# Where the causal mask enters the scores: a product on TensorE, or a copy into the bank by ScalarE

## What is computed

```
q = rmsnorm(q, q_norm_w); k = rmsnorm(k, k_norm_w)
q = apply_rope(q, cos, sin); k = apply_rope(k, cos, sin)
scores = einsum('bhqd,bhkd->bhqk', q, k) * scale
scores = where(causal, scores, finfo.min)
attn = einsum('bhqk,bhkd->bhqd', softmax(scores), v)
hidden = hidden + attn.reshape(B, S, Hq * hd) @ o_w.T
```

## Time and profile before

| | us |
|---|---|
| median of 3 runs | 1182.44 |
| lowest, highest | 1181.94, 1184.58 |
| the profiled execution, its own time | 1183.33 |
| span of the profiled execution, first to last instruction | 1181.4 |
| busy in it: PE | 1144.4 (97%) |
| DVE | 745.2 (63%) |
| ACT | 648.6 (55%) |
| POOL | 509.0 (43%) |
| mask products (L2236), 64 of 0.379 each | 24.2 |

### The profile page before, as it was taken

One profiled execution on the slowest core, in us unless ns is written; L12 is line 12 of the kernel. 1 busy time (PEld: TensorE's weight loads), 2 busy tenths in 40 slices (PEclk: granted clock), 3 DMA queues, 4 the chain that ended last, 5 costly groups with the idle time before them and its releaser, 6 DMA issues.

```text
span 1181.4 us, 22702 instructions
## 1 busy us (share of the span) xinstructions
PE 1144.4 (97%) x7726; PEld 1021.7 (86%) x7726; DVE 745.2 (63%) x1633; ACT 648.6 (55%) x1839; POOL 509.0 (43%) x566
## 2 busy tenths in 40 slices
PE   9999999999999999999999999999999999988994
PEld 8989999999999999998997788888888888867894
DVE  4666545335543454358777877677777777777666
ACT  4555444444444444455565676666666666674552
POOL 4111131113111311312237776666787587673572
PEclk9999999999999999999999999999999999999997
DMA  9200000000000002023002009910000100042637
GB/s 334 85 1 1 19 2 18 1 1 1 1 19 1 1 1 90 1 98 117 19 18 72 1 1 274 291 43 1 15 19 6 50 20 19 15 99 75 197 112 234
DMA packets 47267, 70.09 MB, mean 59 GB/s; under 512 B 4279, under 2 KB 39355, under 8 KB 46171
## 3 DMA queue, kind: packets, MB, share of 16 engines
q1 hardware_dynamic: 43747, 60.21, 16.9%
q0 software_dynamic: 3408, 8.43, 2.0%
HBM read 40.24 MB, written 29.30 MB: 59 GB/s over the span
## 4 chain that ended last, share of the span: by engine, by line
PE 88%; DVE 5%; issue 2%; ACT 2%; POOL 1%; DMA 1%; SPq 0%; DVEq 0%; POOLq 0%; ACTq 0%
PE bank L1904 15%; PE bank L1941 11%; PE bank L2094 10%; PE bank L1972 7%; PE bank L2148 7%; PE bank L1914 5%; PE bank L1932 5%; PE bank L2239 4%; PE bank L2174 4%; PE bank L2034 3%; PE bank L2279 3%; PE bank L1922 2%; PE bank L2204 2%; PE bank L2214 2%; PE bank L2310 2%
## 5 line engine op out<-in xcount | busy, mean ns | idle before, releaser
L600 POOL TENSOR_TENSOR p<-p,rinv 128x512 f32<-128x512 f32 x64 | 66.6, 1041 | 403.6 <-DVE rinv L1430 403.6
L947 ACT ACTIVATE p<-bank,nb,rq 128x128 f32<-128x128 f32 x256 | 114.0, 455 | 87.7 <-DVE nb L1659 87.6
L814 ACT ACTIVATE p<-bank,nmax 128x128 f32<-128x128 f32 x256 | 90.8, 366 | 115.7 <-DVE nmax L1418 115.5
L675 POOL TENSOR_TENSOR qr<-qr,rb 128x512 f32<-128x512 f32 x64 | 82.5, 1289 | 72.1 <-DVE rb L1607 70.6
L1426 DVE COPY pt<-bank 128x512 f32<-128x512 f32 x64 | 44.2, 691 | 106.1 <-PE bank L1922 105.4
L1904 PE MATMUL bank<-cur_hi,wqk_hi 128*128 128x512 f32 x256 | 107.7, 421 | 0.0
L1904 PE MATMUL bank<-cur_lo,wqk_hi 128*128 128x512 f32 x256 | 101.0, 394 | 0.0
L1904 PE MATMUL bank<-cur_hi,wqk_lo 128*128 128x512 f32 x256 | 100.8, 394 | 0.0
L823 ACT ACTIVATE o_hi<-bank,bqkv 128x512 fp32r<-128x512 f32 x64 | 44.3, 692 | 95.7 <-PE bank L1932 95.4
L1434 DVE SCALAR_TENSOR_TENSOR o_lo<-bank,bqkv,o_hi 128x512 fp32r<-128x512 f32 x64 | 48.0, 750 | 49.7 <-ACT o_hi L823 49.7
L1941 PE MATMUL bank<-wo_hi,o_hi 128*128 128x256 f32 x256 | 77.5, 303 | 0.3 <-DVE o_lo L1434 0.2
(11 more groups left out here) (280 smaller groups left out, 3740.8 us busy)
## 6 DMA issues: line engine op xcount, KB each, us to landing
token_scratch<-empty SPq DMA_DIRECT2D x1, 17415.0 KB, 64.9
xs<-token_scratch SPq DMA_DIRECT2D x39, 129.0 KB, 2.2
wqk_raw<-in_wqk SPq DMA_DIRECT2D x8, 512.0 KB, 9.2
gate<-gates_scratch SPq DMA_DIRECT2D x8, 512.0 KB, 3.7
got_t<-expert_scratch SPq DMA_DIRECT2D x16, 256.0 KB, 4.7
w_raw<-in_w SPq DMA_DIRECT2D x2, 1408.0 KB, 6.1
xres<-in_x SPq DMA_DIRECT2D x4, 512.0 KB, 8.8
wv_raw<-in_wv SPq DMA_DIRECT2D x8, 256.0 KB, 9.3
```

Of the source, the lines that this page charges most:

```text
L600: nc.gpsimd.tensor_tensor(p1[:, h % 2], p1[:, h % 2], rinv[:, h % 2].unsqueeze(2).broadcast_to([P, GB, T]), ALU.mult).then_inc(a_pn, 1)
L675: nc.gpsimd.tensor_tensor(qr[:, s.u % 2], qr[:, s.u % 2], rb[:], ALU.add).then_inc(g_qr, 1)
L814: last = nc.scalar.activation(p1[:, h % 2, b], bank[3][:, b * T:(b + 1) * T], ACT.Exp, bias=nmax[:, h % 2, b:b + 1], accum_out=rsum[:, h % ...
L947: last = nc.scalar.activation(p2[:, (s.u - 3) % 2, j], bank[3][:, j * T:(j + 1) * T], ACT.Exp, scale=rq[:, (s.u - 3) % 4, j:j + 1], bias=n ...
```

## The change

The product for the mask is gone, and so are the two tables for it (`mask`, `ident_b`) with the two instructions of DVE that made them. ACT copies `mask_f` (float32, 128 columns, read four times by a stride of 0) into `bank[3]` instead, by `lay_mask`. It does so once ahead of the first scores and then right behind the exponentials of each step, after it has waited for its own last exponential. PE waits for `g_mask` where it waited for `g_ex`, and adds the scores onto what lies in the bank. One product is new (128x512, once, in the first step): its result is overwritten, but it marks the columns of the bank as written, so that later products without `start` add.

```
+            def lay_mask():
+                nc.scalar.activation(bank[3][:].rearrange("p (j s) -> p j s", j=REP),
+                                     mask_f[:].unsqueeze(1).broadcast_to([P, REP, T]), ACT.Copy).then_inc(g_mask, 1)
+
             def step(s):
                 n, new_seq = s.n, s.new() and s.kv == 0
+                if s.first and s.u == 1:
+                    act.wait_ge(consts, 6)
+                    act.wait_ge(g_add, 1)
+                    lay_mask()
...
                     last.then_inc(g_ex, 1)
+                    if n - 2 < NG * 4 * GB:
+                        act.wait_ge(g_ex, n - 2)
+                        lay_mask()
...
-                            dve.wait_ge(consts, 6)
-                            nc.vector.tensor_copy(mask[:].rearrange("p (j s) -> p j s", j=REP),
-                                                  mask_f[:].unsqueeze(1).broadcast_to([P, REP, T])).then_inc(g_tab, 1)
-                            nc.vector.tensor_copy(ident_b[:], ident[:]).then_inc(g_tab, 1)
...
                     keys_queries()
+                    if s.first and s.u == 0:
+                        pe.matmul(bank[3][:], cur_hi[:, 0, 0:T], cur_hi[:, 0], start=True, stop=True).then_inc(g_add, 1)
...
-                    if s.had(3):
-                        pe.wait_ge(g_ex, n - 2)
-
-                    pe.matmul(bank[3][:], ident_b[:], mask[:], start=True, stop=False, skip_group_check=True)
+                    pe.wait_ge(g_mask, n - 1)
```

More of the change, by code:

```diff
@@ L168, in program @@
         cos_sin = sb("cos_sin", [P, 2, DH], at=W2 + 44 * KB)
-        mask = sb("mask", [P, REP * T], BF16, at=W2 + 45 * KB)
-        ident_b = sb("ident_b", [P, P], BF16, at=W2 + 46 * KB)
         mask_f = sb("mask_f", [P, T], at=W2 + 46 * KB + 256)
@@ L313, in program @@
             sem(f"g_{x}") for x in ("ka", "rk", "kv", "qr", "rq", "qv", "pn"))
+        g_mask, g_add = sem("g_mask"), sem("g_add")
         w_hi4, w_lo4 = sem("w_hi4"), sem("w_lo4")
@@ L471, in _ @@
             sp.dma_start(w_row[:], ins["w_row"].partition_broadcast(P)).then_inc(d_router, 16)
-            sp.wait_ge(g_tab, 11)
+            sp.wait_ge(g_tab, 9)
             sp.dma_start(xs_dram.rearrange("(j p) d -> p j d", p=P),
@@ L1595, in _ @@
                 ffn1(g, False)
-            dve.wait_ge(g_tab, 6)
+            dve.wait_ge(g_tab, 4)
             def rotate(out_cos, out_sin, src, table, cos_free, sin_free, done):
@@ L1637, in step @@
                     nc.vector.tensor_copy(iota[:], iota_i[:]).then_inc(g_tab, 1)
-                    dve.wait_ge(g_tab, 8)
+                    dve.wait_ge(g_tab, 6)
                     nc.vector.tensor_scalar(e_base[:], iota[:, 0:E], float(CAP), None, ALU.mult).then_inc(g_tab, 1)
                     nc.vector.tensor_copy(code[:], code_i[:]).then_inc(g_tab, 1)
-                    dve.wait_ge(g_tab, 10)
+                    dve.wait_ge(g_tab, 8)
                     nc.vector.tensor_scalar(e16[:], iota[:, 0:E], float(CAP // P), None, ALU.mult)
@@ L1644, in step @@
                     nc.vector.tensor_copy(empty[:, D + 1:DW], code[:, GB:GB + 1]).then_inc(g_tab, 1)
-                    dve.wait_ge(g_tab, 11)
+                    dve.wait_ge(g_tab, 9)
                 if s.u == 7:
```

## The result

The kernel with the copied mask takes 1188.92 us (median of 6 runs, 1186.85 to 1190.83); the kernel before took 1184.01 (6 runs, 1181.94 to 1184.63). The ratio is 1.0046, with 1.0034 to 1.0059 as its 95% interval: **0.46% slower**, about 5.4 us, where I had forecast no change. It is above my range, which ended at 1187.0, also if the ratio is laid on the 1182.44 that I had then (1187.9). The profiled execution took 1188.24 with a span of 1186.4, 5.0 more than before.

What follows compares the result with a forecast made beforehand. The prediction took PE to set the pace, with 0.22 us saved per step; nine gains and losses along the second attention summed to -0.2 us, so a median of 1182.2, no visible change. Range: 1176.0 to 1187.0, 8 in 10.

Steps and rivals of the forecast that it cites:

- E: End of the last row reading the exponentials' sums, which releases the score bank; scores could start 0.79 us after it.
- clamps: Steps where the score bank is late: scores start 0.43 us later than before instead of 0.22 sooner.
- DVE's ring: Loop `sq`, `q_ms`, `o_lo`, `nmax`, `nb`, exponentials: 5.23 us after the change against PE's 5.46, pacing where DVE has extra work.
- term 8: 1026 to 1048 us, routing and steps without projections: two later `sq` and three clamps against 4 products saved, +2.3 us.
- term 5: 845 to 931 us: 13 steps gain 0.22 each, less two clamps of 0.5 and 0.1, -2.3 us.
- term 7: 966 to 1026 us: 9 steps gain 0.22 each, less one clamp of 0.4, -1.6 us.
- 2, to 743: 693 to 743 us, into the second group: two clamps and DVE's later end against 7 products saved, +0.3 us.
- 4, border to the third: 825 to 845 us: routing and input split in DVE's ring (0.63 late), then two slacks under 0.79, +0.7 us.
- 6, border to the last: 931 to 966 us: DVE builds a list, its ring runs 0.63 longer twice, against 4 products saved, +1.4 us.
- ACT's ring sets the pace everywhere: Rival: copy at its upper bound, 0.9 with wait, makes the ring 5.48, over PE's 5.46: 1186.7 us, chance 0.17.
- The cover holds: Rival: group borders absorb the delay, only first group and end lose, 51 steps keep 0.22: 1175.2 us, chance 0.18.
- term 9: Behind the last scores: `wd_hi` stands behind a copy and the experts' first work waits for it, +0.2 us.

Runs made afterwards that it cites:

- second pair: Traces of the unchanged change, run again (1200.21 us against 1194.11, ratio 1.0049), and of the kernel before (1195.45), on one chip; last scores +3.44 us.
- first pair: Traces of the kernel before and the change from the first measurement (ratio 1.0046); the last scores moved by +5.66 us.
- e10: Kernel before with the copy in 30 steps (groups 2 to 4, steps 0, 4 to 9, 11 to 13), product in 34: 1178.11 us against 1183.06, ratio 0.9956.
- e2: Kernel before with its product, plus ACT copying the mask to an unread spare buffer, PE not waiting: 1200.19 us against 1194.81, ratio 1.0048.
- e3: As e2, with PE also waiting for that copy ahead of the mask's product: 1205.88 us against the kernel before's 1194.81, ratio 1.0097.
- e12: Kernel before with the copy only in steps 18 to 61, 44 of them, the product elsewhere: 1180.27 us against 1183.06, ratio 0.9975.

## Why the prediction was wrong

**Right, by its own steps.** The copy takes 0.602 us (forecast 0.60), and starts 0.03 behind E (0.05); the scores start 0.14 behind it. `sq` is 0.67 later in steps with head 2 or 3 (0.63). PE's step inside a group fell by 0.21 (0.22). From the scores at 744.79 to those at 825.04 before lie 80.25 us; after, 749.00 to 826.99, 77.99: 2.3 nearer (2.7). The waits for the copy are 17 (some 20) with 13.6 us, a little above my 8 to 13.

**Wrong: the sum.** The last scores moved by 3.4 and 5.7 us, over the 2 us that I had named as the sign of being wrong. The mechanism was right: clamps where the bank is late, later `sq` in DVE's ring, gains between. What failed is the price of the late places, in term 8 (forecast +2.3, measured +3.6), term 5 (-2.3, -1.45) and term 7 (-1.6, -1.0). My ledger, against the second pair of traces, in which PE's granted clock is 1.00 from the first scores to the last (start of the scores after minus before, us):

| stretch | forecast | second pair | first pair |
|---|---|---|---|
| 1, first group | +1.5 | +1.9 | +3.55 |
| 2, to 743 | +0.3 | +0.8 | +0.8 |
| 3, to 825 | -2.7 | -2.4 | -2.4 |
| 4, border to the third | +0.7 | +0.5 | +0.5 |
| 5, to 931 | -2.3 | -1.45 | -1.0 |
| 6, border to the last | +1.4 | +1.55 | +1.5 |
| 7, to 1026 | -1.6 | -1.0 | -1.0 |
| 8, to the last scores | +2.3 | +3.6 | +3.7 |
| 9, behind them | +0.2 | +1.0 | -0.7 |

In the second pair no stretch has the wrong sign. But of nine terms, each between 0.2 and 2.7, eight are off to the same side, by 0.15 to 1.3 us, and the sum of gains and losses that nearly cancel moved from -0.2 to +4.4. My forecast's own range, 3 us to either side, fits errors that partly cancel; these did not. Terms 2, 4, 6 and 9 were given without their sums, so that no step of theirs can be called right or wrong, also where they came out near.

**Terms 5 and 7** ("13 x 0.22, less two clamps of 0.5 and 0.1"; "9 x 0.22, less one clamp of 0.4"). I counted 0.6 and 0.4 for late places. Measured, as shift plus the 0.21 not gained, they are 0.60 at step 42, 0.19 at 46 and 0.39 at 47, and 0.83 at step 58. At 42 and 58 the lead that PE has gained shortly before is lost. DVE (its wait, rows and maxima), ACT (end of the exponentials) and PE (scores) around step 42, in the kernel before:

```profile
892.12 1.95 DVE L1103 SCALAR_TENSOR_TENSOR rows<-xres,rstd,w_row 128x256 f32<-128x256 f32 x4 [0.49 <-DMA token_scratch<-rows,index]
893.99 0.68 DVE L1655 TENSOR_REDUCE nmax<-bank 128x4 f32<-128x512 f32 x1
896.63 0.21 ACT L947 ACTIVATION_READ_ACCUMULATOR p<-bank,nb,rq 128x1 f32 x1
897.85 1.05 PE L2239 MATMUL bank<-k_t,q_t 128*128 128x128 f32 x8
```

and in the change, run on the same chip:

```profile
892.15 1.91 DVE L1114 SCALAR_TENSOR_TENSOR rows<-xres,rstd,w_row 128x256 f32<-128x256 f32 x4 [0.61 <-DMA token_scratch<-rows,index]
893.98 0.68 DVE L1662 TENSOR_REDUCE nmax<-bank 128x4 f32<-128x512 f32 x1
896.62 0.21 ACT L955 ACTIVATION_READ_ACCUMULATOR p<-bank,nb,rq 128x1 f32 x1
897.60 1.13 PE L2245 MATMUL bank<-k_t,q_t 128*128 128x128 f32 x8 [0.45 <-ACT bank L932]
```

One step ahead PE was 0.64 early. The maxima come at the same time all the same, and so does E. DVE waits ahead of the maxima, with rows to write, for a transfer that POOL issues, and POOL goes from row to row there without waiting for another engine. In the kernel before:

```profile
875.96 1.26 POOL L675 TENSOR_TENSOR qr<-qr,rb 128x512 f32<-128x512 f32 x1 [1.87 <-DVE rb L1607]
...
889.21 1.06 POOL L647 DMA_INDIRECT token_scratch<-rows,index  x1 [0.18 <-issue]
```

in the change:

```profile
875.96 1.27 POOL L674 TENSOR_TENSOR qr<-qr,rb 128x512 f32<-128x512 f32 x1 [1.66 <-DVE rb L1614]
...
889.20 1.06 POOL L646 DMA_INDIRECT token_scratch<-rows,index  x1 [0.18 <-issue]
```

POOL enters its run at 875.96 in both, at the end of step 38, where PE's shift was 0.00 too, and leaves it at the same time; the 0.64 that PE gains in the next three steps reach neither the maxima nor E. Before, PE had 1.01 us from E to its scores there, and the copy asks for 0.77 of it: so of the lead of 0.64 only 0.25 pass, and the shift goes to -0.25 in place of -0.85. At step 58 (-0.17 to +0.45) it is the same run of POOL, only that it begins 0.70 late (983.33 instead of 982.63): the maxima come 0.67 late, although PE has caught up to -0.17 in the meantime. At 46 and 47 DVE's routing rows stand in the ring, which the later `sq` delays; at 47 `nb` also starts 1.14 behind its maxima's start instead of 0.80, which no row explains. In e10 POOL's run is as much sooner as PE was ahead of it (maxima at 891.53, 2.46 sooner), and PE is 3.08 ahead. But no copy stands at steps 42 and 58, a product needs only 0.14 behind E, and the lead passes: -3.08 still at step 42, and all but 0.2 of it at 58 (-5.01 to -4.78).

**Term 8** (two later `sq` and three clamps: 2 x 0.63 + 3 x 0.43, less one product of 0.22, for a clamp of 0.43 has its own product in it already). From step 63 to 64 alone the loss is 2.0 us, in both pairs and in e2, which has only the load. The end of the exponentials, DVE and POOL there, in the kernel before:

```profile
1039.47 0.68 DVE L1655 TENSOR_REDUCE nmax<-bank 128x4 f32<-128x512 f32 x1
1039.57 0.95 POOL L717 TENSOR_TENSOR w_lo<-w_raw,w_hi 128x352 fp32r<-128x352 f32 x1
1039.57 1.86 POOL L717 TENSOR_TENSOR w_lo<-w_raw,w_hi 128x352 fp32r<-128x352 f32 x2
1040.26 0.28 DVE L1659 TENSOR_TENSOR nb<-nmax,rq 128x4 f32<-128x4 f32 x1
1040.98 0.47 DVE L1220 TENSOR_TENSOR two<-two 128x4 f32<-128x4 f32 x1
1042.23 0.21 ACT L947 ACTIVATION_READ_ACCUMULATOR p<-bank,nb,rq 128x1 f32 x1
1042.80 1.05 PE L2239 MATMUL bank<-k_t,q_t 128*128 128x128 f32 x8
```

in the change, run on the same chip:

```profile
1041.06 1.83 POOL L716 TENSOR_TENSOR w_lo<-w_raw,w_hi 128x352 fp32r<-128x352 f32 x2
1041.26 0.68 DVE L1662 TENSOR_REDUCE nmax<-bank 128x4 f32<-128x512 f32 x1
1042.05 0.86 DVE L1666 TENSOR_TENSOR nb<-nmax,rq 128x4 f32<-128x4 f32 x1
1043.36 0.16 DVE L1231 TENSOR_TENSOR two<-two 128x4 f32<-128x4 f32 x1
1044.60 0.21 ACT L955 ACTIVATION_READ_ACCUMULATOR p<-bank,nb,rq 128x1 f32 x1
1045.59 1.13 PE L2245 MATMUL bank<-k_t,q_t 128*128 128x128 f32 x8 [1.80 <-ACT bank L932]
```

The maxima are 1.79 late: E of the step ahead came 1.14 late, and `sq` 0.66 more. `nb`, a row of 128x4, takes 0.86 instead of 0.28, and ends at 1042.91, 0.02 behind POOL's pair (1041.06 + 1.83 = 1042.89): 0.58 more. E is 2.37 late, and the clamp of 0.42 makes 2.79. I had the `sq` and the clamp, and not `nb`. POOL's pair was there before too, but `nb` met only its first row: it took 0.28 in place of 0.16 undisturbed (at 1049.79 before) and ended at 1040.54, 0.02 behind that row (1039.57 + 0.95). `two`, also of 128x4, shows the reverse: 0.47 before, ending 0.02 behind the pair, and 0.16 in the change, where the pair is over by then. In e2 `nb` takes 0.87 and ends 0.01 behind the pair.

The Trainium skill (SBUF — State Buffer, "Who interferes with whom") says that VectorE and GpSimd share a pair of ports under a lock that one of them holds exclusively, and that a VectorE instruction with two inputs in SBUF contends with a GpSimd instruction that reads SBUF. The ends of `nb` and `two` right at the ends of POOL's rows agree with it, though no run moved POOL's pair by itself.

The same happens two steps earlier, at step 62. In the kernel before:

```profile
1027.99 1.87 POOL L717 TENSOR_TENSOR w_lo<-w_raw,w_hi 128x352 fp32r<-128x352 f32 x2
1028.76 0.21 DVE L1659 TENSOR_TENSOR nb<-nmax,rq 128x4 f32<-128x4 f32 x1
```

in the change:

```profile
1027.97 1.86 POOL L716 TENSOR_TENSOR w_lo<-w_raw,w_hi 128x352 fp32r<-128x352 f32 x2
1029.15 0.69 DVE L1666 TENSOR_TENSOR nb<-nmax,rq 128x4 f32<-128x4 f32 x1
```

The maxima are 0.40 late there, `nb` takes 0.48 more and ends 0.01 behind the pair, and E is 0.88 late. From there on the ring's rows on DVE wait for nothing but the late `sq`, so that the 0.48 stays. At step 65 `nb` takes 0.81 instead of 0.64, 0.17 more. So 0.48 + 0.58 + 0.17 = 1.23 of the 1.3 us that the term was short are `nb`: a row of DVE on the ring that I had left at its length of before.

**The rivals.** "ACT's ring sets the pace everywhere" had the right sign and a near time (1186.7), for a reason that did not hold: the copy is 0.60 and the ring does not bind inside the groups (the step from 763.13 to 768.58 takes 5.45, where it took 5.67, and e2 and e3 lose nothing there). "The cover holds" did not hold for the borders: over the 44 steps of e12 it would give 44 x 0.22 = 9.7 us, of which 3.0 came. Only with the borders left out too (e10, 30 steps) does most of it arrive, 5.2 of 6.6.

**Still open**: the 1.0 us behind the last scores in the second pair against -0.7 in the first (term 9, forecast +0.2; PE has half-speed stretches there in both kernels, at other times), and whether PE's waits make a half-speed stretch more likely. In the first trace of the change there was a second one at 1049.0 to 1052.5 us (granted clock 0.54); neither trace of the kernel before has one between 20 us and there.

## What to carry to other kernels

Work moved from a busy engine to an idle one is paid by the second's place in the dependency ring, not by its busy share: ask at each place which work covers the new instruction and its wait, use it where there is cover (30 of 64 steps, 0.44% faster) and keep the old way where there is none (64 of 64, 0.46% slower). Where another queue sets the time of a place (here POOL's run of 876 to 890 us), the pacing engine can only be ahead of it by its slack there, and an instruction that eats this slack costs its own delay and the lead gained since. And when a forecast is the small difference of large gains and losses, its terms can all err to one side, as eight of nine did here: the range belongs around the sum of their bounds. A small row that shares time with another engine's long rows, such as `nb` here, can change its length when its place moves.

## What the hardware showed that I had not expected

- ACT writes 128x512 from SBUF to PSUM in 0.602 us, from SBUF to SBUF in 0.631 (e2) and from PSUM to SBUF in 0.600: the destination makes 0.03 us. The Trainium skill (ScalarE: Activation LUTs, step-by-step) calls PSUM the faster one; the rows agree in sign, with a difference of no weight here. The next instruction of ACT starts 0.54 behind the copy's start (0.47 to 0.48 behind its neighbours').
- ACT starts 0.03 us behind the end of its own last row if it waits for it (the copy), and 0.10 ahead of that end if it doesn't (`sq` before): the wait takes 0.13.
- A row of DVE of 128x4 with two inputs takes 0.16 us, and up to 0.87 while POOL works on 128x352 rows; it ended 0.01 to 0.02 behind a row of POOL in five cases.
- A bank seeded by ACT and added to by products without `start` worked over 64 uses after one product that wrote all its columns. A seed of 0 and -1e30 was added to, not overwritten.
- One wait of 1.99 us on PE, at the same place in two executions of the same kernel, was followed by 3.5 us at a granted clock of 0.55 in one and by 1.00 in the other.
